# Last batch group of an early-fusion attention and expert block: from two images a step to four heads of one image, with routing and dispatch of the group before moved into the loop

## The reference, cut to what matters

```python
h = tokens(x)                                    # 16x16 patches @ W + b, class token, positions: 37 rows
h = concatenate([h, txt], axis=1)                # 32 images x 114 tokens x 256
n = layernorm(h)
q, k, v = n @ Wq, n @ Wk, n @ Wv                 # 16 heads of 64
a = softmax(causal(q @ k.T / 8)) @ v
h = h + n + a @ Wo
n = layernorm(h)
gates = softmax(n @ router_w + router_b)         # 8 experts
# top 2; each token takes the next free slot of its two experts (cumulative count, capacity 570)
y = sum over its two experts of gate * (gelu(n @ w1 + b1) @ w2 + b2)
return h + y
```

## Time and profile before

| | us |
|---|---|
| median of 3 runs (lowest, highest) | 888.34 (887.63, 888.59) |
| the profiled execution | 888.15 |
| its span | 886.4 |
| PE busy | 841.6 (95%) |
| DVE busy | 563.8 (64%) |
| ACT busy | 508.7 (57%) |
| POOL busy | 375.0 (42%) |
| chain that ended last: share of PE, of DVE | 80%, 11% |

### The profile page before, as it was taken

One profiled execution on the slowest core, in us unless ns is written; L12 is line 12 of the kernel. 1 busy time (PEld: TensorE's weight loads), 2 busy tenths in 40 slices (PEclk: granted clock), 3 DMA queues, 4 the chain that ended last, 5 costly groups with the idle time before them and its releaser, 6 DMA issues.

```text
span 886.4 us, 20329 instructions
## 1 busy us (share of the span) xinstructions
PE 841.6 (95%) x7103; PEld 763.1 (86%) x7103; DVE 563.8 (64%) x2458; ACT 508.7 (57%) x1688; POOL 375.0 (42%) x678
## 2 busy tenths in 40 slices
PE   6799999999999999999999999999579999999996
PEld 6688898888889889888888988988569999999995
DVE  3567438566674855866576486477557877668771
ACT  3477657556674765666467377566055555556551
POOL 2144334254543724544364373465614223441334
PEclk9999999999999999999999999999779999999999
DMA  8333120011003102101200110010446444543322
GB/s 237 100 101 153 44 56 23 2 52 49 24 14 78 33 1 68 44 13 36 60 18 2 38 30 6 9 33 3 122 127 194 110 128 115 126 134 96 69 27 28
DMA packets 55575, 57.69 MB, mean 65 GB/s; under 512 B 26831, under 2 KB 47579, under 8 KB 55360
## 3 DMA queue, kind: packets, MB, share of 16 engines
q1 hardware_dynamic: 34834, 45.15, 16.4%
q0 software_dynamic: 18944, 9.76, 6.9%
q10 hardware_dynamic: 1696, 1.49, 0.6%
HBM read 34.25 MB, written 21.89 MB: 63 GB/s over the span
## 4 chain that ended last, share of the span: by engine, by line
PE 80%; DVE 11%; issue 3%; SPq 2%; DMA 1%; ACT 1%; POOL 1%; POOLq 0%; DVEq 0%
PE bank L409 14%; PE bank L411 14%; PE bank L410 14%; PE o_bank L1324 5%; PE score_bank L1304 5%; PE pT_bank L1313 5%; PE bank L1192 3%; DVE sm L1021 2%; PE o_bank L410 2%; PE o_bank L411 2%; PE o_bank L409 2%; PE score_bank L409 2%; PE score_bank L410 2%; PE score_bank L411 2%; PE bank L1274 1%
## 5 line engine op out<-in xcount | busy, mean ns | idle before, releaser
L598 POOL TENSOR_SCALAR pr<-pr,rc 114x114 f32<-114x114 f32 x512 | 181.0, 370 | 300.9 <-DVE rc L1063 299.8
L740 ACT ACTIVATE pr<-sm,nb 114x114 f32<-114x114 f32 x512 | 192.3, 383 | 7.8 <-DVE nb L1025 7.6
L629 POOL DMA_INDIRECT out_dram<-yout,dest x40 | 74.1, 1852 | 159.9 <-ACT yout L786 158.4
L1021 DVE CUSTOM_DVE_ANT_0 sm<-score_bank,mask 114x114 f32<-114x114 f32 x512 | 109.9, 272 | 49.8 <-PE score_bank L1304 49.7
L409 PE MATMUL bank<-xT_hi,wqkv_hi 128*128 128x456 f32 (+1 forms) x288 | 110.8, 385 | 3.0 <-ACT vv L649 1.7
L734 ACT ACTIVATE pT<-pT_bank 114x456 f32<-114x456 f32 x128 | 70.5, 551 | 53.3 <-PE pT_bank L1313 52.8
L410 PE MATMUL bank<-xT_lo,wqkv_hi 128*128 128x456 f32 (+1 forms) x288 | 100.2, 348 | 0.0
L411 PE MATMUL bank<-xT_hi,wqkv_lo 128*128 128x456 f32 (+1 forms) x288 | 100.1, 348 | 0.0
L740 ACT ACTIVATION_READ_ACCUMULATOR pr<-sm,nb 114x1 f32 x512 | 99.0, 193 | 0.0
L713 ACT ACTIVATE oT_hi<-o_bank 128x228 fp32r<-128x228 f32 x128 | 45.3, 354 | 79.2 <-PE o_bank L1324 69.1
L1313 PE MATMUL pT_bank<-ident,pr 114*114 114x114 f32 x512 | 74.3, 267 | 0.7 <-ACT pT L734 0.7
(11 more groups left out here) (203 smaller groups left out, 2254.7 us busy)
## 6 DMA issues: line engine op xcount, KB each, us to landing
stage_a<-in_L_ffn_w_dram SPq DMA_DIRECT2D x8, 1024.0 KB
stage_b<-in_L_ffn_w_dram SPq DMA_DIRECT2D x8, 1024.0 KB
slots_dram<-fill SPq DMA_DIRECT2D x8, 605.6 KB
pix<-in_x_dram SPq DMA_DIRECT2D x96, 36.0 KB, 2.2
xs<-slots_dram SPq DMA_DIRECT2D x8, 363.4 KB
hraw<-in_txt_dram SPq DMA_DIRECT2D x8, 308.0 KB
out_dram<-h SPq DMA_DIRECT2D x8, 308.0 KB
xs<-slots_dram SPq DMA_DIRECT2D x8, 242.2 KB
```

The costliest lines, as they stand in the source:

```text
L598: p = pool.tensor_scalar(pr[:, m % 4, i, :], pr[:, m % 4, i, :], rc[:, m % 4, i:i + 1], 1.0, ALU.mult, ALU.mult)
L629: pool.indirect_dma_start(out, bass.IndirectOffsetOnAxis(ap=dest[e % 2][:, t:t + 1], axis=0), yout[:, t, :], None, compute_op=ALU.add).the ...
L740: a = act.activation(pr[:, N % 4, i, :], sm[:, N % 2, i, :], ACT.Exp, bias=nb[:, N % 2, i:i + 1], scale=SCALE, accum_out=rs[:, N % 4, i:i ...
L1021: m = dve.tensor_tensor_reduce(sm[:, N % 2, i, :], score_bank[i % 2][0:T, o:o + T], mask[:, :], 1.0, NEG, ALU.add, ALU.max, mx[:, N % 2, i ...
```

## The change

**Order of the last group.** A step is now two chunks of one image: image 0 in steps 0 to 3, image 1 in 4 to 7, image 2 in 8 to 11 and image 3 in 12 to 15. K and Q are projected whole (six matmuls of 456 columns, all four images), one at k = -3, three at k = -2, four each at k = -1, 0 and 1, and six chunks of the eight lie in a new tile `last_qk` over the patch tiles that are no longer used. The scores of a new image or of its second half wait for up to four chunks. All values of the last group are made at k = 2, 3 and 6 to 9, 11 and 12.

**Projections and routing.** `project_last_o` of images 0, 1 and 2 now stands at k = 10, 13 and 17, and only that of image 3 after the loop. Statistics, logits and routing of group 6 stand a step earlier, its slots are made at k = 15 and its eight dispatches follow at k = 15 to 17. The rows of `FIRST_HALF` are transposed at k = 16 and its logits made at k = 17.

```diff
-        ROUTE_LAST = [{14: (0,), 15: (1, 2)}, {12: (0,), 13: (1, 2), 14: (3, 4)}]
+        ROUTE_LAST = [{14: (0,), 15: (1, 2)}, {12: (1, 2), 13: (3, 4)}]
-        AT_HALF_O = 14
+        LAST_O, LAST_Y, LAST_L, LAST_C, ROUTED_C = {10: 0, 13: 1, 17: 2}, 16, 17, 14, 15
+        LAST_DISPATCH = {15: (0, 1), 16: (2, 3, 4), 17: (5, 6, 7)}
+        LAST_QK = {-3: ("K0",), -2: ("Q0", "K1", "Q1"), -1: ("K2", "Q2", "K3", "Q3"), 0: ("K4", "Q4", "K5", "Q5"), 1: ("K6", "Q6", "K7", "Q7")}
+        LAST_V = [{2: 0, 6: 1, 8: 2, 11: 3}, {3: 0, 7: 1, 9: 2, 12: 3}]
 
-            return AT_L if g + 1 != LAST else AT_X
+            return AT_X if g + 1 == LAST else AT_L - (g == LAST)
+        def pace(g, n):
+            return n + (g == LAST)
...
-            return (f, n // 2, 2 * (n % 2)) if f < LAST else (f, n % HP, 2 * (n // HP))
+            return (f, n // 2, 2 * (n % 2)) if f < LAST else (f, 2 * (n % (HP // 2)), n // (HP // 2))
+        def heads_of(m):
+            f, c, b = pair_at(m)
+            return [(c, b), (c, b + 1)] if f < LAST else [(c, b), (c + 1, b)]
...
+        def projected(name, c):
+            w, u = "QK".index(name), c - HP * LAST
+            return last_qk[:, u, w, :] if 0 <= u < HP - 2 else qk[:, w, c % 2, :]
...
-                if N == STEPS:
+                if N == PAIRS * LAST + ROUTED_C - 1:
                     rstd(FIRST_HALF, vareps2, rstd2_done, ve2, rstd2, unit_slice(FIRST_HALF))
-            for i in range(TOPK * GB):
-                if i == TOPK * GB // 2:
-                    rstd(SECOND_HALF, vareps2, rstd2_done, ve2, rstd2, unit_slice(SECOND_HALF))
-                dispatch(LAST - 1, i)
+                for i in LAST_DISPATCH.get(N - PAIRS * LAST, ()):
+                    dispatch(LAST - 1, i)
+            rstd(SECOND_HALF, vareps2, rstd2_done, ve2, rstd2, unit_slice(SECOND_HALF))
...
+                k = N - PAIRS * LAST
+                if k == ROUTED_C:
                     route(LAST - 1, 5)
+                if k == LAST_Y + 1:
+                    drain_y(FIRST_HALF)
+                if k == LAST_L + 1:
+                    route(FIRST_HALF, 0)
...
+                if k == LAST_L + 1:
+                    route(FIRST_HALF, 1)
+                if k - 1 in LAST_O:
+                    add_last(LAST_O[k - 1])
+                if k == ROUTED_C - 1:
+                    last_moments(FIRST_HALF)
+                if k == ROUTED_C:
                     for b in unit_images(FIRST_HALF):
                         normalise_rows(FIRST_HALF, b)
+                if k == LAST_L + 1:
+                    route(FIRST_HALF, 2)
...
-            drain_y(FIRST_HALF)
-            add_last(2)
-            route(FIRST_HALF, 0)
-            route(FIRST_HALF, 1)
+            route(FIRST_HALF, 3)
+            route(FIRST_HALF, 4)
             add_last(3)
             last_moments(SECOND_HALF)
-            route(FIRST_HALF, 2)
-            route(FIRST_HALF, 3)
+            route(FIRST_HALF, 5)
             for b in unit_images(SECOND_HALF):
                 normalise_rows(SECOND_HALF, b)
-            route(FIRST_HALF, 4)
             drain_y(SECOND_HALF)
-            route(FIRST_HALF, 5)
...
-                    for job in (("K", HP * f + c), ("Q", HP * f + c)) if f < LAST else (("QK", N % PAIRS), ("QK", N % PAIRS + 1)):
-                        wait_all(pe, drained(*job))
+                    for d in range(HP * f + c, HP * f + c + (1 if f < LAST else 4)):
+                        wait_all(pe, drained("K", d))
+                        wait_all(pe, drained("Q", d))
...
-                        if 0 <= m < STEPS:
+                        if 0 <= m < STEPS - 1:
                             weigh_values(m)
+                if N == STEPS + LAG_O - 2:
+                    weigh_values(STEPS - 1)
...
+                k = N - PAIRS * LAST
+                if k == LAST_Y:
+                    transpose_tokens("Y", FIRST_HALF, rows[LAST % 2], xn2_done)
+                if k == LAST_L:
+                    logits(FIRST_HALF)
+                if k in LAST_O:
+                    project_last_o(LAST_O[k])
+                if k == LAST_C:
                     count_places(LAST - 1)
-            transpose_tokens("Y", FIRST_HALF, rows[LAST % 2], xn2_done)
-            project_last_o(2)
-            logits(FIRST_HALF)
             project_last_o(3)
+            count_places(FIRST_HALF)
             stay_warm(12)
             transpose_tokens("Y", SECOND_HALF, rows[LAST % 2], xn2_done)
-            count_places(FIRST_HALF)
             logits(SECOND_HALF)
```

147 lines of the change are left out of this document (65 added, 82 removed).

## The result

The changed kernel takes 895.94 us, the median of four executions (893.17 to 897.67); the kernel before takes 888.0 (887.63 to 888.59). The ratio is 1.0085, with a 95% interval of 1.0069 to 1.0101. Measured again with six executions it was 897.86 us, 1.0102 (1.0082 to 1.0122). The forecast was 891.9 and its range ended at 895.4: the sign was right, the size about half. The profiled execution is the slowest of the four: 897.67 us, span 895.9, mean granted clock 0.975, against 888.15, 886.4 and 0.984 before.

What follows compares the result with a forecast made beforehand. PE, busy 95% of the span, was taken as the bound, with DVE's order close at attention's end and POOL third. 4.6 - 1.4 - 1.4 = +1.8, plus 2.0 for the clock, on 888.15 gave 891.9 us; range 885.8 to 895.4.

Steps and rivals of the forecast that it cites:

- Front: Last group up to the scores of step 124: changes in PE's work and waits sum to +3.1 us.
- a half unit: Piece of the old K and Q work on PE: 1.42 us each, fifteen ahead of step 124's scores, 21.3 us.
- The two waits: PE waits for DVE's copy of a Q projection ahead of the scores at k = 0 and 2: +1.9 us.
- DVE's chain: DVE from its start on step 124's scores to the low part of step 122: 12.7 us, ending at 617.5.
- The gap: PE idle ahead of `weigh_values(124)`, waiting for DVE's low part of step 122: about 3 us.
- Gains behind: Behind the last projection: normalised rows sooner, -1.4 us, and POOL free when the last slots are ready, -1.4 us.
- POOL's queue: Dispatches of group 6 gone from the tail, so the last four start right behind their slots: -1.4 us.
- The clock: PE's clock falls ahead of one or both last projections: 0 to 5.8 us more, 2.0 taken; chance 0.50.
- A clock that holds: Rival for the tail: PE's clock does not fall in the new gaps, 889.9 us; chance 0.16.
- The fourth rival: Two POOL dispatches ahead of its scaling of step 127 hold up the tail, up to 2.8 us more, 894.7; chance 0.10.
- The second rival: PE stays filled behind the last scores: 886.6 us, or 885.4 if both waits are hidden; chance 0.16.
- the second gap: PE idle ahead of the last projection, with DVE waiting for `ex` in between: 3 us.

Runs made afterwards that it cites:

- the second profile: Profile of the changed kernel, unaltered, when it was timed once more beside the follow-up kernels; that execution took 898.13 us, the median 897.86.
- old_tail: Changed kernel up to its last scores, with everything behind them put back as in the kernel before; 889.72 us, ratio 1.0015.
- old_tail_swap: `old_tail` with PE's `weigh_values` ahead of the scores at k = 0 and 2; 887.36 us, ratio 0.9987.
- fill_first: Changed kernel with ten unread products on PE in the gap ahead of `weigh_values(124)`; 894.02 us, ratio 1.0069.
- low_fill1: `low_both` with five unread products in what is left of its first gap; 891.53 us, ratio 1.0042.
- fill_early: Changed kernel with eight unread products in each of the two gaps, on the next job's bank; 892.69 us, ratio 1.0045.
- o_late: Changed kernel with output projections of images 0 and 1 at k = 14 and 15, transposes and logits one step later; 897.96 us.
- o_late_pool: `o_late` with POOL's dispatches of group 6 behind `rstd` instead of two ahead of its scaling of step 127; 895.08 us, ratio 1.007.
- low_both: Changed kernel with DVE's low parts ahead of routing and `add_last` work, and POOL's first `rstd` one step later; 896.52 us, ratio 1.0092.
- low_fill: `low_both` with ten unread products ahead of the last output projection; 895.79 us, ratio 1.0076.
- tail_best: `old_tail_swap` with group 6's places one step earlier and one of its dispatches ahead of `rstd`; 887.17 us, ratio 0.9983.

## Why the prediction was right in its sign and wrong in its size

**Front.** Forecast 603.6 for the scores of step 124, measured 604.12; in the second profile they stand at 605.84, mostly by the earlier fall of the clock, for which the forecast had no term. The 1.42 us that it calls a half unit are a whole one, as its count of fifteen needs. The two waits were forecast at 0.93 and are 0.92. That they lie on the path is shown by the pairs with the products exchanged, `old_tail` and `old_tail_swap` above all.

**DVE's chain.** Forecast 12.7 us up to the low part of step 122, measured 12.96 + the 1.13 in front of it, which ends at 618.21 instead of 617.5. The gap was forecast at 3 and is 2.78. The second was forecast at 3 and is 2.80; `es` waits 0.92 us for `ex` ahead of it as described.

**Gains behind.** 2.22 us to the normalised rows, as forecast. For POOL's queue I had taken 1.4, the distance of one dispatch; the trace gives 1.70 - 1.05 = 0.65. In return the last slots came 0.47 sooner behind the rows; 0.28 of it are the logits of the second half, whose products took 0.94 us where they took 1.22 before. Together 2.5 instead of 2.8.

**The clock: the step that failed.** The forecast took 2.0 us out of a bound of 0 to 5.8, and the bound itself counted only the two projections. From `weigh_values(124)` to the transposes of step 127 the forecast has 624.3 - 617.5 = 6.8 us, and the trace 629.54 - 618.35 = 11.19, **4.4 more**, 2.5 of it in the projection of image 2 and the rest in transposes and logits, which I had left at full clock. From the start of the last projection to DVE taking it, it has 3.16 and the trace 639.64 - 634.40 = 5.24, **2.1 more**. Together 6.5, where 2.0 was taken. With the first gap ending 0.85 late (618.35 for 617.5), 0.25 more in front of the second and 0.3 less gain behind it, 1.8 + 4.4 + 2.1 + 0.85 + 0.25 + 0.3 = 9.7, against the 9.66 measured at the last dispatches. The reason that I gave for so small a share, that a projection may start low and recover under its own work, was wrong for image 2: its products ran low throughout (5.38 us for 2.89), and the clock was back only when they were over, at 629. In the second profile a share of the clock comes out smaller but well over 2.0 too, with these two projections at 4.61 + 4.42 - 2.89 - 2.90 = 3.2 us over full clock. The Trainium skill's rule in "TensorE: Matmul & The Clock Gate", Part 1, that "activity releases the throttle", agrees with the fills of `fill_first` and `low_fill1`: with added products alone the clock was back near 620 and 621 instead of 629 and 627. It spoke against the change, and more so than I let it.

**The rivals.** A clock that holds was to give 889.9. Where the profile shows it held behind the last scores, in `fill_early`, that execution took 892.5 us, and the median is 892.7. So this rival was 2 to 3 us too fast. About 0.9 of that is the `rstd` behind the dispatches; the rest was not settled. The fourth rival, POOL's two dispatches ahead of the scaling of step 127, did not show in the changed kernel, where PE asks for it late; in `o_late` it cost 2.3 us of the gap of 3.57, since 1.28 were left in `o_late_pool`. The second rival, a PE that stays filled, was to be decided by DVE's 12.7 us (by its own terms its lower value is 888.15 + 1.2 - 1.9 - 2.8 = 884.7, not 885.4, which moves no other number). `low_both` took 1.6 us of the 2.78 us gap away by DVE's order, and the time did not move: what PE lacks there is work.

**What the change costs, taken apart.** By medians: the front 889.72 - 888.2 = 1.5 us; the hoist of two projections 895.32 - 889.72 = 5.6; the rest of the new tail 897.86 - 895.32 = 2.5, these last two kernels measured beside one another. Against the changed kernel's first measurement (895.94) the rest is 0.6, and the intervals overlap, so it lies somewhere between nothing and some 4 us. I had laid the loss on DVE's order behind the last scores. The runs lay most of it on the hoist: the projections of images 0 and 1 were the dense work that stood beside the chain of masks, exponentials, scaling and copies. Moved ahead of the last scores they delay that chain by their own length, and leave PE with short products and waits, in which the clock falls. How much of the rest is clock and how much order stays open.

## What to carry to other kernels

Dense work that stands beside a latency-bound chain pays twice when it is moved ahead of the chain's start: it delays the chain, and it leaves the engine idle enough for the clock to fall. Price such a gap as the idle time plus everything on TensorE that may run at half clock behind it, small operations included, and not as the idle time alone; here that was 10 us of work, from 619 to 629, the whole of the next projection with it. If the gap can't be closed, a few unread products in it are a cheap repair (4 to 5 us here for five of them). Their place mattered more than their number: ten in the second gap (`low_fill`) gained nothing that could be told from noise.

## What the runs showed of the hardware that I had not expected

The granted clock fell behind a gap of 1.17 us in `low_both` as behind one of 2.78, while the kernel before kept 1.00 with gaps of 0.73, 0.64 and 0.44 around its projections. The length of a gap alone does not tell it: `old_tail` kept 1.00 behind a gap of 1.08 with two projections next, and in the second profile of the changed kernel the clock fell at 534 to 540 behind no gap longer than 0.55. The same fill ran at full clock in one kernel's profile (2.50 us for twenty rows) and in part at half clock in another's (3.98), though both kernels are the same up to there: where exactly the clock falls differs from execution to execution.

POOL's fourth dispatch of group 6 starts behind 2.4 us or more of idle time, where most of its neighbours wait 0.30, whatever stands around it. It is 2.44 us before (at 625.35), 2.43 in `tail_best`, 3.22 in `old_tail` and 3.58 in `fill_early`, and in the changed kernel

```profile
627.61 1.14 POOL L611 DMA_INDIRECT slots_dram<-rows,slot  x1 [2.45 <-issue]
```

No run here says why.
